# Gram products of a tile in one run, other TensorE work spread over a slot per unit, lookups written straight into the gram operand

## Chip, cores and metric

One core of one Trainium2 chip. The metric is the device time of one execution in microseconds, the median of several runs. TensorE is called PE, VectorE DVE, ScalarE ACT, GpSimd POOL, SyncE SP.

## What is computed

For 2048 samples, 32 table rows of 256 values each are gathered by `ids`; all dot products of two different rows of a sample (496) and 16 dense values make 512 features, and three dense layers follow:

```python
e = jnp.stack([tbl_0[ids[:, 0]], ..., tbl_31[ids[:, 31]]], axis=1)   # [2048, 32, 256]
dots = jnp.einsum('bnd,bmd->bnm', e, e)[:, iu, ju]                   # pairs i < j: 496
h = jnp.concatenate([dots, dense_ctx], axis=1)                       # [2048, 512]
h = jnp.maximum(h @ W_top1 + b_top1, 0.0)                            # 512
h = jnp.maximum(h @ W_top2 + b_top2, 0.0)                            # 256
y = h @ W_top3                                                       # [2048, 1]
```

The tables have 1000, 1250 or 12500 rows; everything is float32.

## The kernel before

**Tiles.** The samples are worked on in 16 tiles of 128. For each tile the kernel needs `turned`: the 32 rows of each sample with the 256 values across the partitions (two chunks of 128), from which `gram` (line 348) forms, for each sample, the products of its 32 rows with 31 of them, 256 small matmuls (512 on PE, as each float32 matmul is issued as two) into two banks of `quad_ps`.

**Two ways into `turned`.** 26 fields come by gather: POOL issues one indirect DMA per field and tile (line 295) into a ring of nine places in `rows`, two fields to a place, called a unit; 13 units make a tile (tile 0 has 15, as three more fields are gathered there). `turn` (line 313) transposes a unit on PE in four steps into a ring of four banks, and ACT or DVE (`ACT_UNITS`) copies the bank into `turned`. The gather of unit n waits until unit n-9 is turned. The other six fields, with 1000 rows each, are looked up: the table stays in SBUF as the sum of a high and a low part (`small`), DVE builds `one_hot` from the ids, and `look_up` (line 326) multiplies both, 32 matmuls for one field and two tiles, into the one bank `look_ps`. ACT copies the bank to `ahead` (line 490), and `place` (line 501) copies it from there into `turned`, twice per tile. There are 48 lookups, three per tile; half the fields come in even tiles, half in odd ones, a tile ahead of their use.

**The split.** In tile 0 ACT writes a table's high part (line 555), copies it to PSUM in four pieces (line 561), and DVE subtracts each piece from the table to get the low part (line 664).

**After gram.** `unfold` (DVE, line 618) moves the products to SBUF, `pick` (ACT, lines 506 to 514) sorts them into `features`, PE transposes these (`turn_features`), `keep_features` copies, then `layer1` (line 407), `keep_hidden1`, `layer2` (line 420) on PE and `last_layers` on DVE.

**Order on PE, written out by hand.** For each tile t: the turns of units 4 to 12, with the features of tile t-1 after unit 6, then layer 1 of tile t-1 (`turn_all`); then eight portions, each a ninth of the tile's lookups followed by an eighth of its gram products; layer 2 of tile t-1 stands after the first portion, and after portions 3 to 6 stand the turns of units 0 to 3 of tile t+1 (`EARLY_AFTER`). A last ninth of the lookups closes the tile. The last tile has a gram of its own (`last_gram`, line 377: 256 matmuls on PE in four banks), and behind it stand its features, layers and the output. ACT, DVE and SP have loops of their own in matching order, bound to PE by semaphores.

Of the kernel before, what the change touches and what calls it, by code (L numbers as in the profile page):

```python
# [8 lines left out]
D = 256  # L9
P = 128  # L10
# [28 lines left out]
def dlrm_tower(nc, dense_ctx, ids, small_ids, tables, w1, b1, w2, b2, w3, out):  # L39
# [30 lines left out]
    ACT_UNITS = [0, 1, 2, 6, 8, 10, 12]  # L70
    RING = 4


    LOOK_AFTER = [2, 5, 8, 11]
    SPLIT_AFTER = [0, 2, 5, 8]

    EARLY_AFTER = [3, 4, 5, 6]

    TURN_FEATURES_AFTER = 6
    PARTS = 8  # L80
    GPP = GROUPS // PARTS
# [7 lines left out]
    AT_ONCE = 2  # L89
    STEPS = SUB // AT_ONCE  # L90
    IDS_RING = 3
    OUTS = 4 * CHUNKS

    LOOKUPS, FIRST = [], {}
    for step in range(-1, TILES):
        FIRST[step] = len(LOOKUPS)
        n = step + 1  # L100
        if step == -1:
            LOOKUPS += [(f, 0, 2) for f in range(EVENS)] + [(EVENS, 1, 2)]
        elif n < TILES and n % 2 == 0:
            LOOKUPS += [(f, n, 2) for f in range(EVENS)]
        elif n < TILES:
            LOOKUPS += [(f, n, min(2, TILES - n)) for f in range(EVENS + (n == 1), SMALL)]
    FIRST[TILES] = len(LOOKUPS)
    PRODUCTS = CHUNKS * SUB * 2

    ctx = ExitStack()  # L110
    with ctx:
# [16 lines left out]
        with nc.sbuf_tensor("landed", [SP, SMALL, SUB, 2, D], fp32) as landed:  # L128
# [4 lines left out]
        ahead = sbuf("ahead", [P, SMALL, CHUNKS, 2 * P])  # L133
# [13 lines left out]
        turn_ps = [psum(f"turn_ps{i}", [P, 512]) for i in range(RING - 2)] + [quad_ps[:, b, :] for b in (2, 3)]  # L147
        look_ps = psum("look_ps", [P, 512])
# [8 lines left out]
        last_h1 = [top_ps, look_ps, turn_ps[0], turn_ps[1]]  # L157
# [7 lines left out]

        high_ps = [bank[0:SP, 0:AT_ONCE * D].rearrange("p (r d) -> p r d", r=AT_ONCE)
                   for bank in (gram_ps[:, 1, :], top_ps)]
# [13 lines left out]
        high_copied = sem("high_copied")  # L181

# [4 lines left out]
        look_kept = sem("look_kept")  # L187
        placed = sem("placed")
# [38 lines left out]
        def n_gathered(n):  # L227

            return 16 * sum(len(UNITS[m][1]) for m in range(n % PLACES, n + 1, PLACES))

# [7 lines left out]
        def _(sp):  # L238
# [71 lines left out]
        def _(pe):  # L310
# [15 lines left out]
            def look_up(n, first, end):  # L326

                f, _, tiles = LOOKUPS[n]
                width = tiles * P
                if first == 0:  # L330
                    pe.wait_ge(one_hot_made, n + 1)
                    if n < SMALL:
                        pe.wait_ge(low_parts, (f + 1) * STEPS)
                    if n > 0:
                        pe.wait_ge(look_kept, n)
                for k in range(first, end):
                    c, r, part = k // (2 * SUB), k // 2 % SUB, k % 2
                    last = pe.matmul(look_ps[:, c * width:(c + 1) * width],  # L338
# [5 lines left out]
            def gram(t, portion):  # L344
                if portion == 0:
                    pe.wait_ge(act_kept, n_act_kept(BEGIN[t + 1] - 1))
                    pe.wait_ge(dve_kept, n_dve_kept(BEGIN[t + 1] - 1))
                    pe.wait_ge(placed, 2 * t + 1)
                    if t > 0:
                        pe.wait_ge(unfolded, t)  # L350
                if t == 0 and portion == PARTS // 2:
                    pe.wait_ge(low_parts, SMALL * STEPS)
                for g in range(portion * GPP, (portion + 1) * GPP):
# [7 lines left out]
                if portion == PARTS - 1:  # L361
                    last.then_inc(gram_done, 1)

            def last_gram(portion):
                t = TILES - 1
# [13 lines left out]
                if (portion + 1) * GPP % LAST_GROUPS == 0:  # L379
                    last.then_inc(last_gram_done, 1)  # L380
# [356 lines left out]
```

## Time and profile before

| | us |
|---|---|
| median of 3 runs | 566.03 (565.94 to 626.95) |
| profiled execution, span | 890.7 |
| PE busy in it | 601.0 |
| POOL busy in it | 398.0 |
| DVE, ACT busy in it | 225.9, 204.6 |

The time of the profiled execution itself is known by its span alone, from the first to the last instruction. A line of the page or of an answer gives an engine, the line of the kernel, the operation, what it writes and reads, how many instructions, and times in us (ns where so marked). "issue" is idle time of an engine for which the profile shows no wait. The span is far longer than the timed runs, which has to be kept in mind with every share.

### The profile page before, as it was taken

The page shows a single profiled execution, that of the slowest core. Times are in us where ns is not written, and L with a number is a line of the kernel's source. Part 1 is how long each engine was busy: PE and PEld are TensorE (multiplying, and loading weights), DVE is VectorE, ACT ScalarE, POOL GpSimd, SP SyncE. Part 2 cuts the span into 40 slices and gives each one's busy share as a digit, 9 for nine tenths or more (in the row PEclk, how much of TensorE's full clock was granted, in tenths as well). Part 3 has the DMA queues.
Part 4 walks back from the last instruction along what each step waited for, and adds up shares of the span by engine and source line. Part 5 has one row for each costly group of instructions (what it writes and reads, how often), then busy time and mean ns, then how long its engine had stood idle before and what let it go on. Part 6 is the DMA issues. An engine that isn't in the chain of part 4 may idle for free.

```text
span 890.7 us, 24184 instructions
## 1 busy us (share of the span) xinstructions
PE 601.0 (67%) x11019; PEld 524.1 (59%) x11019; DVE 225.9 (25%) x578; ACT 204.6 (23%) x369; POOL 398.0 (45%) x426
## 2 busy tenths in 40 slices
PE   3557668486684867748577584875848668486687
PEld 2456557375572756737467474765737657375586
DVE  3444313123130231402223032231312313123122
ACT  4252303103030030401313022130210303103042
POOL 7563625526255361543715347262462625526220
PEclk9688969698796987969789697896969969698799
DMA  9962312313122141321313224131231312313110
GB/s 220 243 204 68 99 42 77 94 44 102 43 78 83 50 107 38 83 73 56 108 37 87 63 57 118 32 96 49 70 105 39 101 41 76 88 41 90 43 38 2
DMA packets 37459, 70.97 MB, mean 80 GB/s; under 512 B 10382, under 2 KB 23438, under 8 KB 37358
## 3 DMA queue, kind: packets, MB, share of 16 engines
q0 software_dynamic: 20112, 54.95, 22.1%
q1 hardware_dynamic: 17246, 14.48, 7.0%
q8 instruction: 87, 1.43, 0.7%
q14 instruction: 14, 0.11, 0.0%
HBM read 69.39 MB, written 0.01 MB: 78 GB/s over the span
## 4 chain that ended last, share of the span: by engine, by line
PE 42%; another core or an unknown queue 30%; issue 13%; ACT 12%; DMA 1%; DVE 1%; POOL 1%; ACTq 0%; DVEq 0%
PE look_ps L338 18%; PE quad_ps L358 12%; PE top_ps L420 6%; ACT turned L501 4%; ACT turned L483 3%; PE turn_ps L322 3%; PE quad_ps L322 2%; ACT area L550 2%; ACT ahead L490 1%; DMA rows<-in_tbl,row_ids 1%; PE quad_ps L377 1%; POOL rows L295 1%; PE top_ps L407 1%; ACT products L506 0%
## 5 line engine op out<-in xcount | busy, mean ns | idle before, releaser
L295 POOL DMA_INDIRECT rows<-in_tbl,row_ids x419 | 397.2, 948 | 458.1 <-PE turn_ps L322 184.1
L338 PE MATMUL look_ps<-one_hot,small 125*128 125x256 f32 (+1 forms) x1536 | 251.9, 303 | 104.7 <-issue 92.8
L338 PEld LDWEIGHTS look_ps<-one_hot,small 125*128 125x128 f32 x1536 | 214.0, 202 | 116.6 <-issue 112.3
L358 PE MATMUL quad_ps<-turned 128*32 128x31 f32 x7680 | 140.0, 204 | 121.8 <-issue 121.5
L358 PEld LDWEIGHTS quad_ps<-turned 128*32 128x32 f32 x7680 | 108.8, 115 | 166.9 <-issue 153.3
L674 DVE TENSOR_SCALAR one_hot<-ids_across,sub_row 125x256 fp32r<-125x256 int32 (+1 forms) x384 | 112.0, 364 | 145.8 <-PE look_ps L338 126.6
L322 PE MATMUL turn_ps<-ident,rows 128*128 128x128 f32 x424 | 64.5, 282 | 28.5 <-issue 14.7
L655 DVE TENSOR_TENSOR top_ps<-top_ps,b_sb 128x256 f32<-128x256 f32 x15 | 6.5, 433 | 299.8 <-PE top_ps L420 299.8
L490 ACT ACTIVATE ahead<-look_ps 128x512 f32<-128x512 f32 (+1 forms) x48 | 28.3, 590 | 232.5 <-PE look_ps L338 219.1
L407 PE MATMUL top_ps<-area,w_sb 128*128 128x128 f32 x488 | 61.9, 276 | 19.5 <-issue 18.8
L550 ACT ACTIVATE area<-top_ps,b_sb 128x128 f32<-128x128 f32 x61 | 17.5, 368 | 227.5 <-remote 225.2
L407 PEld LDWEIGHTS top_ps<-area,w_sb 128*128 128x128 f32 x488 | 57.8, 192 | 18.1 <-issue 17.2
L322 PEld LDWEIGHTS turn_ps<-ident,rows 128*128 128x128 f32 x424 | 48.2, 143 | 31.8 <-issue 28.2
L483 ACT ACTIVATE turned<-turn_ps 128x512 f32<-128x512 f32 x57 | 35.0, 631 | 114.2 <-PE quad_ps L358 76.2
L322 PE MATMUL quad_ps<-ident,rows 128*128 128x128 f32 x414 | 60.1, 279 | 0.8 <-DMA rows<-in_tbl,row_ids 0.8
L483 ACT ACTIVATE turned<-quad_ps 128x512 f32<-128x512 f32 x55 | 33.9, 631 | 90.6 <-PE quad_ps L358 70.8
L420 PE MATMUL top_ps<-w_sb,area 128*128 128x256 f32 x120 | 49.4, 585 | 4.1 <-ACT area L550 4.1
L618 DVE STREAM_TRANSPOSE products<-quad_ps 128x992 f32<-128x992 f32 x15 | 18.3, 1217 | 127.7 <-PE quad_ps L358 127.7
L322 PEld LDWEIGHTS quad_ps<-ident,rows 128*128 128x128 f32 x414 | 46.5, 142 | 2.9 <-DMA rows<-in_tbl,row_ids 1.2
L501 ACT ACTIVATE turned<-ahead 128x768 f32<-128x768 f32 x31 | 45.0, 1552 | 0.0
L420 PEld LDWEIGHTS top_ps<-w_sb,area 128*128 128x128 f32 x120 | 35.6, 311 | 13.9 <-ACT area L550 6.1
L609 DVE COPY turned<-quad_ps 128x512 f32<-128x512 f32 (+1 forms) x49 | 33.0, 681 | 34.1 <-PE quad_ps L322 14.6
(50 smaller groups left out, 169.9 us busy)
## 6 DMA issues: line engine op xcount, KB each, us to landing
rows<-in_tbl,row_ids POOLq DMA_INDIRECT x419
ids_across<-in_small_ids SPq DMA_DIRECT2D x45, 128.0 KB
landed<-in_tbl SPq DMA_DIRECT2D x6, 896.0 KB
w_sb<-in_W_top SPq DMA_DIRECT2D x4, 256.0 KB
landed<-in_tbl SPq DMA_DIRECT2D x6, 104.0 KB
w_sb<-in_W_top SPq DMA_DIRECT2D x1, 512.0 KB
area<-in_dense_ctx SPq DMA_DIRECT2D x16, 8.0 KB
row_ids<-in_ids SPq DMA_DIRECT2D x1, 240.0 KB
```

Source lines behind the costliest of these rows:

```text
L295: pool.indirect_dma_start(out=rows[:, n % PLACES, j, :], out_offset=None, in_=tables[f], in_offset=bass.IndirectOffsetOnAxis(ap=row_ids[:, ...
L322: last = pe.transpose(turn_ps[n % RING][:, at:at + P], rows[:, n % PLACES, j, c * P:(c + 1) * P], ident[:, :])
L338: last = pe.matmul(look_ps[:, c * width:(c + 1) * width], small[:, f, r, part, c * P:(c + 1) * P], one_hot[n % 2][:, r, 0:width], start=(r ...
L358: last = pe.matmul(gram_ps[q * FIELDS:(q + 1) * FIELDS, g // BANK_GROUPS, at:at + COLS], turned[:, c, s, :], turned[:, c, s, 0:COLS], star ...
L407: last = pe.matmul(bank[:, m * P:(m + 1) * P], w1_sb[:, c, m * P:(m + 1) * P], features_t[:, c, :], start=(c == 0), stop=(c == KC - 1))
L420: last = pe.matmul((last_h2 if t == TILES - 1 else top_ps)[:, 0:HIDDEN2], hidden1[:, c, :], w2_sb[:, c, :], start=(c == 0), stop=(c == M1 ...
L483: act.activation(turned[:, :, :, f:f + len(unit)], turn_ps[n % RING][:, 0:CHUNKS * len(unit) * P].rearrange("p (c f s) -> p c s f", c=CHUN ...
L490: act.activation(ahead[:, f, :, 0:tiles * P], look_ps[:, 0:CHUNKS * tiles * P].rearrange("p (c s) -> p c s", c=CHUNKS), ACT.Copy).then_inc ...
L501: act.activation(turned[:, :, :, fs].rearrange("p c s f -> p f c s"), ahead[:, fs, :, half * P:(half + 1) * P], ACT.Copy).then_inc(placed, 1)
L550: act.activation(hidden1[:, m, :], bank[:, m * P:(m + 1) * P], ACT.Relu, bias=b1_sb[:, m:m + 1]).then_inc(h1_kept, 1)
L609: dve.tensor_copy(turned[:, :, :, f:f + len(unit)], turn_ps[n % RING][:, 0:CHUNKS * len(unit) * P].rearrange("p (c f s) -> p c s f", c=CHU ...
L674: last = dve.tensor_scalar(one_hot[n % 2][:, r, 0:width], ids_across[0:SP, n % IDS_RING, 0:width], sub_row[:, r:r + 1], None, ALU.is_equal)
```

## The change

PE's order becomes: for each tile t from 1 on, 13 slots, one per unit. A slot turns the unit, then does its share of the tile's lookups (`SLOT_SHARES`, 96 matmuls in all); slot 2 also transposes the features of tile t-1, slots 5 to 8 do a quarter of layer 1 each, slot 12 does layer 2 (slot 10 in the last tile). Then the gram products of tile t follow in one run. Tile 0 has its turns and three lookups, then gram. Turn banks go from four to three, lookup banks from one to two. A lookup is copied by ACT straight into `turned` for its own tile, and its second tile's half to `ahead`, so that `place` runs once per tile. The split of a small table is one copy on ACT and one subtraction on DVE with both operands in SBUF, spread over tile 0. ACT's, DVE's and SP's loops follow the slots. POOL's program is as before. The core of the diff:

```diff
-    ACT_UNITS = [0, 1, 2, 6, 8, 10, 12]
-    RING = 4
-    EARLY_AFTER = [3, 4, 5, 6]
-    TURN_FEATURES_AFTER = 6
-    PARTS = 8
+    ACT_UNITS = [0, 2, 4, 6, 8, 10, 12]
+    RING = 3
+    LOOKS = 2
+    LOOK_AFTER = [2, 5, 8]
+    HIGH_AFTER = [0, 2, 5, 8, 10, 12]
+    LOW_AFTER = [0, 2, 5, 9, 11, 13]
+    FEATURES_SLOT = 2
+    LAYER1_SLOTS = [5, 6, 7, 8]
+    LAYER2_SLOT = 12
+    LAST_LAYER2_SLOT = 10
+    SLOT_SHARES = [11, 11, 7, 11, 11, 3, 3, 3, 3, 11, 11, 11, 0]
...
+    for t in range(TILES):
+        FIRST[t] = len(LOOKUPS)
+        LOOKUPS += [(f, t, min(2, TILES - t)) for f in (range(EVENS) if t % 2 == 0 else range(EVENS, SMALL))]
...
-            load_ids(5)
             for t in range(TILES):
-                if t + 2 in FIRST:
-                    for n in range(FIRST[t + 1], FIRST[t + 2]):
-                        load_ids(n)
-                if t + 1 < TILES:
-                    load_dense(t + 1)
+                for n in range(FIRST[t], FIRST[t + 1]):
+                    if t > 0 and n == FIRST[t + 1] - 1:
+                        load_dense(t)
+                    if n >= 2 and n + 3 < len(LOOKUPS):
+                        load_ids(n + 3)
...
+            gram(0)
+            for t in range(1, TILES):
+                for i in range(BEGIN[t + 1] - BEGIN[t]):
+                    turn(BEGIN[t] + i)
+                    look_in_slot(t, i)
+                    if i == FEATURES_SLOT:
+                        turn_features(t - 1)
+                    if i in LAYER1_SLOTS:
+                        layer1(t - 1, LAYER1_SLOTS.index(i))
+                    if i == (LAST_LAYER2_SLOT if t == TILES - 1 else LAYER2_SLOT):
                         layer2(t - 1)
-                    if k in EARLY_AFTER and t + 1 < TILES:
-                        turn(BEGIN[t + 1] + EARLY_AFTER.index(k))
-                look_between(t, PARTS)
+                if t < TILES - 1:
+                    gram(t)
+                else:
+                    last_gram()
...
-                act.activation(ahead[:, f, :, 0:tiles * P],
-                               look_ps[:, 0:CHUNKS * tiles * P].rearrange("p (c s) -> p c s", c=CHUNKS),
-                               ACT.Copy).then_inc(look_kept, 1)
+                both = look_ps[n % LOOKS][:, 0:CHUNKS * tiles * P].rearrange("p (c t s) -> p t c s", c=CHUNKS, t=tiles)
+                act.activation(turned[:, :, :, f], both[:, 0, :, :], ACT.Copy).then_inc(look_placed, 1)
+                if tiles == 2:
+                    act.activation(ahead[:, f, :, :], both[:, 1, :, :], ACT.Copy).then_inc(look_kept, 1)
...
-                act.wait_ge(high_ready, i + 1)
-                for k in range(STEPS):
-                    n = i * STEPS + k
-                    if n >= 2:
-                        act.wait_ge(low_parts, n - 1)
-                    act.activation(high_ps[n % 2], small[:, i, k * AT_ONCE:(k + 1) * AT_ONCE, 0, :],
-                                   ACT.Copy).then_inc(high_copied, 1)
...
             def split_low(i):
-                for k in range(STEPS):
-                    n, part = i * STEPS + k, slice(k * AT_ONCE, (k + 1) * AT_ONCE)
-                    dve.wait_ge(high_copied, n + 1)
-                    dve.tensor_tensor(small[:, i, part, 1, :], landed[:, i, part, 1, :], high_ps[n % 2],
-                                             ALU.subtract).then_inc(low_parts, 1)
+                dve.wait_ge(high_ready, i + 1)
+                dve.tensor_tensor(small[:, i, :, 1, :], landed[:, i, :, 1, :], small[:, i, :, 0, :],
+                                  ALU.subtract).then_inc(low_parts, 1)
...
+            for t in range(1, TILES):
+                unfold(t - 1)
+                for i in range(BEGIN[t + 1] - BEGIN[t]):
+                    if i not in ACT_UNITS:
+                        keep_turned(BEGIN[t] + i)
+                    for n in done_in_slot(t, i):
+                        if n + 2 < len(LOOKUPS):
+                            make_one_hot(n + 2)
+                    if t == TILES - 1 and i == LAST_LAYER2_SLOT:
                         last_layers(t - 1)
-                if t == TILES - 1:
+                if t < TILES - 1:
                     last_layers(t - 1)
```

ACT's loop, not shown, does per tile: `place`, then in each slot the unit's copy if it is ACT's, the lookups that ended in that slot, `pick` in slot 0, `keep_features` in slot 2 and `keep_hidden1` in slot 8.

## Rows read from the trace of the kernel before

**Rows 1.** The page's head.
```profile
span 890.7 us, 24184 instructions
```
**Rows 2.** Cores: span and mean granted TensorE clock.
```profile
core 0: 890.7 us, clock 0.850
```
**Rows 3.** List of waits: engine, output, line, releaser; us, times, longest.
```profile
PE quad_ps L358 <- issue: 121.5, 188, 1.9
...
PE look_ps L338 <- issue: 92.8, 103, 2.0
```
**Rows 4.** Stretches: length, busy PE, PEld, DVE, ACT, POOL; clock, DMA share, GB/s.
```profile
377.00:394.00 17.00, 4.88 (x17) 3.33 (x18) 0.82 (x3) 0.60 (x1) 10.84 (x12) 0.63 0.38 107
...
407.00:421.00 14.00, 10.45 (x290) 8.90 (x288) 2.33 (x8) 0.60 (x1) 7.05 (x8) 1.00 0.25 71
```
**Rows 5.** Timeline of POOL: start, us, instruction, idle time before and its releaser.
```profile
2.71 1.10 POOL L295 DMA_INDIRECT rows<-in_tbl,row_ids  x1 [1.15 <-DMA row_ids<-in_ids]
4.12 0.95 POOL L295 DMA_INDIRECT rows<-in_tbl,row_ids  x1 [0.30 <-issue]
...
389.00 0.95 POOL L295 DMA_INDIRECT rows<-in_tbl,row_ids  x1 [0.30 <-issue]
390.25 0.95 POOL L295 DMA_INDIRECT rows<-in_tbl,row_ids  x1 [0.30 <-issue]
406.38 0.94 POOL L295 DMA_INDIRECT rows<-in_tbl,row_ids  x1 [15.19 <-PE turn_ps L322]
...
855.87 0.95 POOL L295 DMA_INDIRECT rows<-in_tbl,row_ids  x1 [0.31 <-issue]
```
**Rows 6.** Timeline of PE, dense stretch of tile 6.
```profile
400.35 0.76 PE L358 MATMUL quad_ps<-turned 128*32 128x31 f32 x64
401.05 1.58 PE L338 MATMUL look_ps<-one_hot,small 125*128 125x256 f32 x11
402.55 0.76 PE L358 MATMUL quad_ps<-turned 128*32 128x31 f32 x64
```
**Rows 7.** Timeline of PE, the last tile.
```profile
862.93 1.04 PE L322 MATMUL turn_ps<-ident,rows 128*128 128x128 f32 x8
863.80 3.74 PE L407 MATMUL top_ps<-area,w_sb 128*128 128x128 f32 x32
867.47 1.15 PE L377 MATMUL quad_ps<-turned 128*64 128x62 f32 x32
868.77 1.99 PE L420 MATMUL top_ps<-w_sb,area 128*128 128x256 f32 x8 [0.15 <-ACT area L550]
870.70 6.75 PE L377 MATMUL quad_ps<-turned 128*64 128x62 f32 x224
```
**Rows 8.** DMA from 855 to 862 us: busy tenths in 40 slices.
```profile
DMA  0030000995100096530000000000000000000000
```
**Rows 9.** Instruction groups by shape: busy us, mean ns of one; idle before.
```profile
L501 ACT ACTIVATE turned<-ahead 128x768 f32<-128x768 f32 x31 | 45.0, 1552 | 0.0
L483 ACT ACTIVATE turned<-turn_ps 128x512 f32<-128x512 f32 x57 | 35.0, 631 | 114.2 <-PE quad_ps L358 76.2 <-remote 24.8 <-PE turn_ps L322 11.3
...
L490 ACT ACTIVATE ahead<-look_ps 128x512 f32<-128x512 f32 x45 | 27.1, 603 | 217.8 <-PE look_ps L338 204.5 <-remote 13.4
...
L512 ACT ACTIVATE area<-products 128x465 f32<-128x465 f32 x15 | 9.2, 612 | 0.5
L664 DVE TENSOR_TENSOR small<-landed,quad_ps 125x512 fp32r<-125x512 f32 x12 | 8.2, 685 | 9.6 <-issue 4.7 <-ACT quad_ps L561 4.5
```
**Rows 10.** Timelines of DVE and POOL: DVE instructions with a gather beside them.
```profile
17.45 0.69 DVE L664 TENSOR_TENSOR small<-landed,quad_ps 125x512 fp32r<-125x512 f32 x1
...
17.87 0.94 POOL L295 DMA_INDIRECT rows<-in_tbl,row_ids  x1 [0.30 <-issue]
...
411.48 2.33 DVE L674 TENSOR_SCALAR one_hot<-ids_across,sub_row 125x256 fp32r<-125x256 int32 x8 [6.55 <-PE look_ps L338]
411.58 1.07 POOL L295 DMA_INDIRECT rows<-in_tbl,row_ids  x1 [0.30 <-issue]
```

More of the change, by code:

```diff
@@ L87, in dlrm_tower @@
     LAST_GROUPS = GROUPS // LAST_BANKS
-    AT_ONCE = 2
-    STEPS = SUB // AT_ONCE
     IDS_RING = 3
-    OUTS = 4 * CHUNKS
     LOOKUPS, FIRST = [], {}
[L98 to L106, printed above, removed]
+    for t in range(TILES):
+        FIRST[t] = len(LOOKUPS)
+        LOOKUPS += [(f, t, min(2, TILES - t)) for f in (range(EVENS) if t % 2 == 0 else range(EVENS, SMALL))]
     FIRST[TILES] = len(LOOKUPS)
     PRODUCTS = CHUNKS * SUB * 2
+    SLOT_ENDS = [sum(SLOT_SHARES[:i + 1]) for i in range(len(SLOT_SHARES))]
     ctx = ExitStack()
@@ L229, in n_gathered, with n_kept, lookups_done, done_in_slot @@
             return 16 * sum(len(UNITS[m][1]) for m in range(n % PLACES, n + 1, PLACES))
+        def n_kept(n):
+            return sum(tiles == 2 for _, _, tiles in LOOKUPS[:n])
+        def lookups_done(t, products):
+            return [n for n in range(FIRST[t], FIRST[t + 1]) if (n + 1 - FIRST[t]) * PRODUCTS <= products]
+        def done_in_slot(t, i):
+            made = (FIRST[t + 1] - FIRST[t]) * PRODUCTS
+            ends = [made * end // SLOT_ENDS[-1] for end in [0] + SLOT_ENDS]
+            return [n for n in lookups_done(t, ends[i + 1]) if n not in lookups_done(t, ends[i])]
         def n_ids(n):
@@ L329, in look_up @@
                 width = tiles * P
+                bank = look_ps[n % LOOKS]
                 if first == 0:
@@ L342, in look_up, with all_in_place, gram @@
                     last.then_inc(looked_up, 1)
[L344 to L353, printed above, removed]
+            def all_in_place(t):
+                pe.wait_ge(act_kept, n_act_kept(BEGIN[t + 1] - 1))
+                pe.wait_ge(dve_kept, n_dve_kept(BEGIN[t + 1] - 1))
+                pe.wait_ge(look_placed, FIRST[t + 1])
+                if t > 0:
+                    pe.wait_ge(placed, t)
+                    pe.wait_ge(unfolded, t)
+            def gram(t):
+                all_in_place(t)
+                for g in range(GROUPS):
                     at = g % BANK_GROUPS * COLS
@@ L360, in gram, with last_gram @@
                                              start=(c == 0), stop=(c == CHUNKS - 1))
[L361 to L365, printed above, removed]
[L366 to L371 removed]
+                last.then_inc(gram_done, 1)
+            def last_gram():
+                all_in_place(TILES - 1)
+                for g in range(GROUPS):
                     at = g % LAST_GROUPS * WIDE
@@ L427, in keep_running, with look_in_slot @@
                     pe.matmul(spare_ps[:, :], ident[:, :], w1_sb[:, 0, :], start=True, stop=True)
-            def turn_all(t):
-                for i in range(len(EARLY_AFTER), BEGIN[t + 1] - BEGIN[t]):
-                    turn(BEGIN[t] + i)
-                    if i == TURN_FEATURES_AFTER:
-                        turn_features(t - 1)
-                for m in range(M1):
-                    layer1(t - 1, m)
-            def look_between(t, k):
-                made = FIRST[t + 1] - FIRST[t]
-                for n in range(made):
-                    begin, end = (n * (PARTS + 1) + made - 1) // made, ((n + 1) * (PARTS + 1) + made - 1) // made
-                    if begin <= k < end:
-                        look_up(FIRST[t] + n, PRODUCTS * (k - begin) // (end - begin),
-                                PRODUCTS * (k + 1 - begin) // (end - begin))
+            def look_in_slot(t, i):
+                made = (FIRST[t + 1] - FIRST[t]) * PRODUCTS
+                begin, end = (made * at // SLOT_ENDS[-1] for at in ([0] + SLOT_ENDS)[i:i + 2])
+                for n in range(FIRST[t], FIRST[t + 1]):
+                    base = (n - FIRST[t]) * PRODUCTS
+                    first, stop = max(begin - base, 0), min(end - base, PRODUCTS)
+                    if first < stop:
+                        look_up(n, first, stop)
             pe.wait_ge(ident_ready, 1)
```

113 lines of the change are left out of this document (35 added, 78 removed).

## The prediction

> **What bounds the kernel now.** I read the page's head first. The profiled execution spans 890.7 us and the median of the timed runs is 566.03, so 324.7 us of the profile are not in the timed runs, and differences inside the profile cannot be carried over as they stand [rows 1]. The list of waits says where they are: PE sat idle with nothing to wait for ("issue") for 121.5 us before gram products and 92.8 us before lookups [rows 3]. The table of stretches shows it inside one tile: from 377 to 394 us PE is busy 4.88 of 17 us at a granted clock of 0.63, and from 407 to 421 us 10.45 of 14 at 1.00 [rows 4]. I take these stalls to come with the recording and rebuild the time from stretches without them.
>
> Two engines could set the end. The Pool queue's timeline: in every unbroken stretch a gather starts 1.25 us after the one before it (389.00, 390.25), 0.95 busy and 0.30 between. It stops only where it waits for a turn that frees a place in `rows`; the 15.19 us before 406.38 is such a wait, and behind it stands the stalled PE [rows 5]. There are 419 gathers: 29 for tile 0, 26 for each later one. A later tile so costs Pool at least 26 x 1.25 = 32.5 us.
>
> PE's tile at the rates of its dense stretches: 52 transposes of 13 units at 0.87 us per 8 = 5.7; four for the features 0.4; layer 1 from 863.80 to 867.47 = 3.7; layer 2 from 868.77 to 870.70 = 1.9 [rows 7]; 96 lookups at 1.50 per 11 = 13.1; eight gram portions at 0.70 = 5.6 [rows 6]. Sum 30.4 us, which is 2.1 under Pool's 32.5.
>
> The whole time by Pool: the first gather starts at 2.71; with 1.41 to the second, the last starts at 2.71 + 1.41 + 417 x 1.25 = 525.4. In the trace the last gather is issued at 855.87 [rows 5], and the view of DMA from 855 to 862 us has its last busy slice (the 18th of 0.175 us) ending at 858.15: landing 2.3 us after the start [rows 8]. So 527.7, the last unit's turn 0.44, layer 1 3.67, then 890.7 - 867.47 = 23.2 for the rest [rows 1, 7]. Sum 555.0. The median is 11.0 above it. Part of that may lie around the span, between launch and end, part may be gaps in Pool's queue; no row divides it.
>
> So I hold that in the timed runs the gathers set the pace and PE waits about 2 us in each tile for the last unit to land.
>
> **Does Pool stay unbroken before?** Gather of unit n needs turn n-9. With E the end of a tile's last gather, layer 1 and four portions (2.2 us each, layer 2 in the first) bring the first early turn to about E + 1.05 + 0.44 + 3.7 + 10.7 + 0.44 = E + 16.3, and Pool asks for it at E + 22.5; the fourth follows at E + 24.3 for E + 30. Some 6 us are spare.
>
> **The change, part by part.**
> *Gram in one run, turns and lookups in 13 slots.* The count of PE instructions is the same. A slot with 11 lookups is 0.44 + 1.50 = 1.94 us, the 13 slots are 30.4 - 5.6 = 24.8, then gram 5.6. Units land every 2.5 us, so PE catches up behind each gram and waits at the end of the tile, now in small pieces. Gram ends near E + 1.05 + 0.44 + 1.9 + 5.6 = E + 9.0 and the next tile's first turn at E + 9.4, where Pool asks at E + 22.5: 13 us spare instead of 6. Worth nothing while Pool was unbroken. If it was not, it is worth what the gaps were, at most the 11.0. I take nothing.
>
> *A ring of three turn banks and two lookup banks.* A turn waits for the copy three units back: 0.63 us long [rows 9], at least three slots of 1.77 us earlier even while PE catches up. A lookup no longer waits for the copy of the one before. Both lie under Pool: nothing. Without that cover a missed copy would cost PE up to 0.63 per unit, 8 us a tile.
>
> *Lookups straight into `turned`.* ScalarE now makes two copies of 256 elements (0.4 to 0.7 us each, between half the 512-element copy's rate and that of `place`, 1552 ns per 768 [rows 9]) in place of one, and one `place` per tile in place of two. Per tile before 3 x 0.6 + 2 x 1.55 = 4.9, after at most 3 x 1.4 + 1.55 = 5.8, of 32.5 us. Behind it queue `keep_turned` and `pick`; `place`, the first turn copy and `pick` (four copies, the longest 0.61) take at most 1.55 + 0.63 + 2.4 = 4.6 us after gram, and `turn_features` asks after 1.94 + 1.94 + 1.4 = 5.3. Covered: nothing.
>
> *SP's queue.* The id lists are still asked for three lookups ahead and the dense block at the tile's last lookup; behind the dense load's wait for `turn_features` (slot 2) stands one id list that is wanted three lookups, a whole tile, later. Nothing. `make_one_hot` moves between VectorE's turn copies: 8 instructions, 2.33 us [rows 10], less than one unit of Pool, three times a tile. Nothing.
>
> *Layers leave the end.* In the last tile layer 1 of tile 14 (3.67) stood between the last turn and the last gram, and layer 2 (1.93) inside that gram. Now they sit in slots 5 to 8 and 10. What comes in their place: the copy of the last unit, formerly under layer 1, now bare (0.63 and about 0.2 to be seen = 0.85). And slot 10 grows to 0.44 + 1.50 + 1.93 = 3.87, with slot 11 5.81 us where two units land in 5.0: 0.8 late. 3.67 + 1.93 - 0.85 - 0.8 = 4.0 us saved (3.95, rounded). This is on the path.
>
> *The split of the small tables.* Before, ScalarE copied the high part to PSUM in four pieces and VectorE subtracted four times (685 ns each, one operand in PSUM). Now VectorE subtracts once, 2048 elements, at most 4 x 0.685 = 2.74 us [rows 9], six times, all during tile 0. Both operands lie in SBUF, a form that the trace of before never shows beside a gather. Lower bound of what it costs Pool: nothing, since the PSUM form runs beside gathers that stay at 0.94 to 0.95 (17.45 and 17.87). Upper bound: Pool stands still throughout, 6 x 2.74 = 16.4 us. The nearest row is a VectorE instruction fed from SBUF alone: where `make_one_hot` starts at 411.48, the gather at 411.58 takes 1.07 instead of 0.95 [rows 10]. I take 0.12 six times = 0.7 us. The Trainium skill speaks against this edit ("SBUF — State Buffer", Who interferes with whom): a VectorE instruction with two SBUF inputs contends with a GpSimd instruction that reads SBUF, and the later of the two is blocked outright, though the same section infers that descriptor writing escapes. By the strict reading the sum would be that of the upper bound, by the inference that of the lower; no row here decides.
>
> **Sum.** Against the rebuilt 555.0: -4.0 + 0.7 = 551.7. The 11.0 us stay, as Pool's program is untouched: 562.7 us, 0.6% under the median.
>
> **Rivals.**
> *Pool was broken before* (0.20). PE's dense 30.4 is near 32.5; a little more per tile in truth, and early turns would come late. Then the change gives the gaps back, at most all 11.0: 551.7. For it: the two sums are 2.1 us apart, and PE is the one engine whose rate the profile disturbs. Against it: the 6 us of spare, and that some of the 11.0 should lie around the span, where nothing can be given back.
> *The split holds Pool* (0.10). Place: tile 0, six subtractions. 566.0 - 4.0 + 16.4 = 578.4. It decides from 4.0 / 6 = 0.67 us per split: above that the kernel is slower than before. For it: the gather stretched to 1.07. Against it: that is an eighth of a gather, not a standstill, and the subtractions of before left the gathers beside them at their length.
> *PE's clock drops as it idles in every slot* (0.04). It decides where the mean granted clock falls under 30.4 / 32.5 = 0.94. At the profile's mean of 0.850 [rows 2] PE's tile is 35.8, 3.3 over Pool: 14 x 3.3 = 46, so 608. Against it: from 407 to 421 us PE was idle a quarter of the time at 1.00 [rows 4], and here it idles one part in fifteen.
> *The change does nothing* (0.04): the end is not shortened because PE reaches the last tile late. 566 to 570.
>
> **How the numbers follow.** Forecast 562.7 us, chance 0.62, its own range 557 to 568. About 2% is what a measurement can tell from no change: under 554.7 is faster, over 577.4 slower. Faster 0.20 (the first rival), same 0.66 (forecast and the last), slower 0.14 (the split, the clock). For 8 in 10 the range takes in the first rival and most of the way to the second: 550 to 575.
>
> **What the profile after would show.** Gathers still 1.25 us apart where unbroken, and none longer than 1.1 beside the new subtraction (2.1 to 2.7 us long): else the second rival. The last gram following the last turn within about 1 us, with no layer 1 or 2 behind it, and some 21.3 us from its start to the end of the span, formerly 23.2. Granted clock at 1.00 wherever PE is not stalled. A time at or under 552 would mean that Pool did not set the pace before; one over 578 that the split or PE's order does so now. The weakest point is that the bound is inferred from rates inside a profile that ran 1.57 times as long as the runs.

## The result and the profile after

The changed kernel takes 650.41 us (646.25 to 654.98, four runs), the kernel before 565.99 beside it: 84.4 us more. The ratio of the fast runs is 1.1527 [1.1458, 1.1596]; it leaves out one run of the kernel before that took 626.95 us (the medians as they stand give 1.149). The prediction said 562.7 and no change; it was wrong. The profiled execution of the changed kernel took 654.98 us, 1.8 more than its span; the other three took 646 to 651, so the loss is not that of one recording.

From the page of the kernel after: the span, the engines' busy time (PEld is PE's weight loads), the queue q8 that carries instructions (packets, MB, share), and the chain that ended last by engine.

```profile
span 653.2 us, 24171 instructions
PE 534.5 (82%) x11019; PEld 507.8 (78%) x11019; DVE 230.5 (35%) x560; ACT 187.5 (29%) x374; POOL 407.8 (62%) x426
q8 instruction: 87, 1.43, 0.9%
PE 78%; issue 15%; POOL 5%; DMA 1%; DVE 0%; ACT 0%; DVEq 0%
```

PE carries the chain, and 15% of the chain is PE idle with no wait that the profile shows. The list of waits (total us, times, longest) says where; it answers to [rows 3]:

```profile
PEld quad_ps L362 <- issue: 104.5, 111, 3.7
PE quad_ps L362 <- issue: 84.8, 47, 3.3
POOL rows L296 <- PE turn_ps L323: 61.2, 34, 6.8
```

L362 is the gram run; 47 idle times, 84.8 us, of which 3.3 stand ahead of the first run and 81.5 inside the 15 runs. PE's timeline over one run and the start of the next tile (start, length, instructions, idle before); it answers to [rows 6]:

```profile
319.64 1.89 PE L418 MATMUL top_ps<-w_sb,area 128*128 128x256 f32 x8
321.46 2.64 PE L362 MATMUL quad_ps<-turned 128*32 128x31 f32 x181
325.78 2.14 PE L362 MATMUL quad_ps<-turned 128*32 128x31 f32 x128 [1.68 <-issue]
329.79 1.93 PE L362 MATMUL quad_ps<-turned 128*32 128x31 f32 x128 [1.86 <-issue]
333.24 1.28 PE L362 MATMUL quad_ps<-turned 128*32 128x31 f32 x75 [1.52 <-issue]
334.45 1.12 PE L323 MATMUL turn_ps<-ident,rows 128*128 128x128 f32 x4
335.22 2.69 PE L341 MATMUL look_ps<-one_hot,small 125*128 125x256 f32 x11
```

The run takes 12.99 us, where the prediction had 5.6. Its first 181 matmuls take 2.64 us, 0.93 per 64 where the prediction had 0.70, and from the 181st on it stops after exactly 128 matmuls each time. Each matmul has a weight load of its own, so 128 matmuls are 256 instructions; and q8 moves 1.43 MB in 87 packets, 16 KB each, against 2 x 11019 matmuls and weight loads, 253 to a packet. Four of these packets fall into this run ("q8 instruction: 4, 0.07, 2.3%" in the view of DMA from 321.46 to 334.45).

The table of stretches: us, then busy time with instructions of PE, PEld, DVE, ACT and POOL, then granted clock, DMA share and GB/s. The rows are the slots before the run, the run, the start of the slots behind it, and the rest of those.

```profile
299.65:321.46 21.81, 21.81 (x175) 21.32 (x174) 10.86 (x29) 7.91 (x17) 16.16 (x17) 0.95 0.41 115
321.46:334.45 12.99, 7.73 (x513) 6.95 (x513) 1.34 (x6) 0.00 (x0) 6.65 (x7) 0.66 0.37 97
334.45:342.00 7.55, 7.55 (x50) 7.55 (x48) 1.91 (x2) 3.75 (x7) 4.25 (x5) 0.69 0.20 55
342.00:359.65 17.65, 17.65 (x148) 17.16 (x147) 10.35 (x29) 7.24 (x16) 13.38 (x15) 1.00 0.44 121
```

PE stops, and the granted clock is at its lower level (1.2 GHz of 2.4) for part of the run and of what follows: 0.66 in the mean of the run, 0.69 in the 7.55 us behind it, 1.00 after that. The 11 lookups at 335.22 take 2.49 us to the next start instead of the 1.50 of [rows 6]. Over 15 tiles the run lasts 13.3 us in the mean, with three stops (four in one run), 5.4 us, in it; the slots between two runs last 24.8. Together 38.1 us a tile against POOL's 32.5 [rows 5]: 15 x 5.6 = 84 us, as much as the measured difference. POOL now waits for PE in nearly every tile:

```profile
329.23 0.95 POOL L296 DMA_INDIRECT rows<-in_tbl,row_ids  x1 [0.30 <-issue]
335.84 0.95 POOL L296 DMA_INDIRECT rows<-in_tbl,row_ids  x1 [5.67 <-PE turn_ps L323]
```

### The profile page after: what moved, and what is told of

It reads as the page before. It is cut to its first block, busy times and chain, and to the rows that moved or that the text cites. A ratio compares the mean times of both kernels' runs of the same rounds, so it can differ in the third digit from the quotient of the medians.

```text
span 653.2 us, 24171 instructions
## 1 busy us (share of the span) xinstructions
PE 534.5 (82%) x11019; PEld 507.8 (78%) x11019; DVE 230.5 (35%) x560; ACT 187.5 (29%) x374; POOL 407.8 (62%) x426
## 3 DMA queue, kind: packets, MB, share of 16 engines
q8 instruction: 87, 1.43, 0.9%
## 4 chain that ended last, share of the span: by engine, by line
PE 78%; issue 15%; POOL 5%; DMA 1%; DVE 0%; ACT 0%; DVEq 0%
PE quad_ps L362 17%; PE quad_ps L341 15%; PE look_ps L341 14%; PE turn_ps L323 10%; PE top_ps L405 9%; PE quad_ps L323 5%; POOL rows L296 5%; PE top_ps L418 4%; PE quad_ps L375 1%; PE top_ps L395 1%; DMA rows<-in_tbl,row_ids 1%; PE turn_ps L405 0%; PE quad_ps L418 0%; DMA row_ids<-in_ids 0%; DVE products L607 0%
## 5 line engine op out<-in xcount | busy, mean ns | idle before, releaser
L362 PE MATMUL quad_ps<-turned 128*32 128x31 f32 x7680 | 115.1, 219 | 88.3 <-issue 84.8
L362 PEld LDWEIGHTS quad_ps<-turned 128*32 128x32 f32 x7680 | 100.2, 131 | 106.3 <-issue 104.5
L341 PE MATMUL look_ps<-one_hot,small 125*128 125x256 f32 (+1 forms) x768 | 130.1, 316 | 0.0
L341 PE MATMUL quad_ps<-one_hot,small 125*128 125x256 f32 (+1 forms) x768 | 127.4, 311 | 0.0
L341 PEld LDWEIGHTS look_ps<-one_hot,small 125*128 125x128 f32 x768 | 112.6, 216 | 0.0
L341 PEld LDWEIGHTS quad_ps<-one_hot,small 125*128 125x128 f32 x768 | 110.0, 212 | 0.0
L323 PE MATMUL turn_ps<-ident,rows 128*128 128x128 f32 x560 | 95.5, 298 | 17.3 <-DMA rows<-in_tbl,row_ids 17.3
L583 DVE COPY turned<-turn_ps 128x512 f32<-128x512 f32 x65 | 45.3, 697 | 123.8 <-PE turn_ps L323 123.6
L323 PEld LDWEIGHTS turn_ps<-ident,rows 128*128 128x128 f32 x560 | 71.4, 153 | 19.8 <-issue 11.4
L491 ACT ACTIVATE turned<-ahead 128x768 f32<-128x768 f32 x15 | 23.3, 1555 | 214.6 <-PE quad_ps L362 214.6
L418 PE MATMUL top_ps<-w_sb,area 128*128 128x256 f32 x120 | 28.4, 380 | 0.0
```

The costliest lines, as they stand in the source:

```text
L323: last = pe.transpose(turn_ps[n % RING][:, at:at + P], rows[:, n % PLACES, j, c * P:(c + 1) * P], ident[:, :])
L341: last = pe.matmul(bank[:, c * width:(c + 1) * width], small[:, f, r, part, c * P:(c + 1) * P], one_hot[n % 2][:, r, 0:width], start=(r == ...
L362: last = pe.matmul(gram_ps[q * FIELDS:(q + 1) * FIELDS, g // BANK_GROUPS, at:at + COLS], turned[:, c, s, :], turned[:, c, s, 0:COLS], star ...
L418: last = pe.matmul((last_h2 if t == TILES - 1 else top_ps)[:, 0:HIDDEN2], hidden1[:, c, :], w2_sb[:, c, :], start=(c == 0), stop=(c == M1 ...
L491: act.activation(turned[:, :, :, fs].rearrange("p c s f -> p f c s"), ahead[:, fs, :, :], ACT.Copy).then_inc(placed, 1)
L583: dve.tensor_copy(turned[:, :, :, f:f + len(unit)], turn_ps[n % RING][:, 0:CHUNKS * len(unit) * P].rearrange("p (c f s) -> p c s f", c=CHU ...
```

## The experiments

The theory that they test: PE's instructions arrive in blocks of 256 (128 short matmuls) at a pace of about one block in 3.7 us, and a run of short matmuls uses them up faster. Rivals: the slots and lookups, the split of the tables, or the end are the cause; or the stops belong to the start of a run. The comparisons stand beside the kernel before on the same chip: 563.98 us for e1 to e4, 562.67 for e5 to e8, 563.82 for e9 and e10, 562.65 for e11 (medians of 9 to 17 runs, which spread over 3 to 7 us). The kernels of e1 to e3, e6 to e8 and e10 were run once each.

### e1: the kernel before, again

No edit; its first profile spans 890.7 us, with PE held up [rows 1, 3, 4].

> The kernel before, unchanged, profiled once more. Theory (the recording stalled the first profile; the timed runs are dense): span about 564 us, PE's idle time marked issue far under the 248 us of the first profile, a tile every 32.5 to 33.5 us, and the gathers 1.25 us apart nearly without a break. Rival (a tile of the kernel before takes the 54.6 us of the first profile in every recorded run): span near 890 us again.

Measured: 559.83 us. The page's head; POOL's last gathers; PE around two portions of gram:

```profile
span 558.0 us, 24184 instructions
PE 507.1 (91%) x11019; PEld 466.4 (84%) x11019; DVE 231.4 (41%) x578; ACT 203.7 (37%) x369; POOL 397.6 (71%) x426
```

```profile
526.54 0.95 POOL L295 DMA_INDIRECT rows<-in_tbl,row_ids  x1 [0.30 <-issue]
527.79 0.95 POOL L295 DMA_INDIRECT rows<-in_tbl,row_ids  x1 [0.30 <-issue]
```

```profile
312.61 0.99 PE L358 MATMUL quad_ps<-turned 128*32 128x31 f32 x64
313.52 1.57 PE L338 MATMUL look_ps<-one_hot,small 125*128 125x256 f32 x11
315.02 0.99 PE L358 MATMUL quad_ps<-turned 128*32 128x31 f32 x64
```

The gathers run unbroken at 1.25 us (2.3 us of gaps in all), so POOL sets the pace, as the prediction held. A portion of 64 with its 11 lookups is 150 instructions in 2.41 us, 62 per us. A block of 256 per 3.7 us is 69 per us. The kernel before lies just under what the supply gives. What held PE up in its first profile is not shown: there PE stops after every one or two matmuls, not 256 instructions apart.

### e2: the kernel before with its gram portions in one run

```diff
-                for k in range(PARTS):
+                for k in range(PARTS + 1):
                     look_between(t, k)
+                    if t > 0 and k == 0:
+                        layer2(t - 1)
+                for k in range(PARTS):
                     if t < TILES - 1:
                         gram(t, k)
...
+                if t + 1 < TILES:
+                    for i in range(len(EARLY_AFTER)):
+                        turn(BEGIN[t + 1] + i)
```

> The kernel before with one thing of the change alone: the lookups of a tile come first, then its gram products in one run, then the four early turns. Lookup path, banks, split and everything else as before. Theory (a run of 512 gram matmuls outruns the supply of PE's instructions): gram takes 12 to 14 us per tile instead of some 6 with stops of 1.7 to 2.2 us after every 128 matmuls, the clock falls to 1.2 GHz behind it, and the time is 640 to 680 us. Rival (slots, three turn banks or the new lookup copies cost the 84 us): about 566 us, at most 575.

Measured: 794.08 us. PE's and POOL's timelines:

```profile
301.31 2.18 PE L358 MATMUL quad_ps<-turned 128*32 128x31 f32 x234
305.74 1.29 PE L358 MATMUL quad_ps<-turned 128*32 128x31 f32 x128 [2.25 <-issue]
309.20 1.93 PE L358 MATMUL quad_ps<-turned 128*32 128x31 f32 x128 [2.16 <-issue]
```

```profile
314.79 0.94 POOL L295 DMA_INDIRECT rows<-in_tbl,row_ids  x1 [16.55 <-PE turn_ps L322]
```

The same stops with the lookup path, banks and split of before: the run in one piece is enough. The size was missed. Here the early turns come only behind the run, the nine places of `rows` fill, and POOL waits for PE 247 us in all, some 16 us a tile; in the changed kernel it is 91 us, some 6 a tile.

### e3: the kernel after with half as many, wider gram instructions

```diff
...
-                        for q in range(QUADS):
-                            s = q * FIELDS + g
-                            last = pe.matmul(gram_ps[...], turned[:, c, s, :], turned[:, c, s, 0:COLS],
+                        for h in range(HALVES):
+                            s = QUADS * g + 2 * h
+                            pair = turned[:, c, s:s + 2, :]
+                            last = pe.matmul(quad_ps[...], pair.rearrange("d s f -> d (s f)"), pair[:, :, 0:COLS],
```

It takes two samples to one matmul, as the last tile does, and writes the products of one half of the samples over those of the other.

> The changed kernel with gram of tiles 0 to 14 in the form of the last tile's: 256 matmuls of 62 columns in place of 512 of 31, so half the instructions in one run, with more array time (7.7 us instead of 4.3). Results of different samples are written over each other, so the output is not the reference's. Theory (instruction supply): no stops of over 1 us within gram, gram 7.7 to 8.5 us, clock back at 2.4 GHz, a tile of some 32.5 us set by the gathers or just above, 555 to 585 us. Rival (the products themselves, the clock or the wait for data make the run slow): gram stays at 12 us or over and the time at 640 us or over.

Measured: 564.82 us.

```profile
314.57 7.68 PE L363 MATMUL quad_ps<-turned 128*64 128x62 f32 x256
```

No stop inside a run, the granted clock at 1.00 in the run shown, tiles of 32.5 us, and the whole loss is gone with the slots, direct lookups, rings and split of the change all in place. The run's 512 instructions (256 matmuls and as many weight loads) take 7.6 us, 67 per us, just under the 69 of the supply. The one thing altered is the number and length of the gram instructions.

### e4: the kernel before with the new split

One copy on ACT and one subtraction on DVE per table, in the places of the old ones (`AT_ONCE` 8, the copies to PSUM left out).

> The kernel before with the new split alone: one copy on ACT and one subtraction on DVE with both operands in SBUF per small table, at the places of before. In the changed kernel's trace the six gathers beside these subtractions took 2.17 to 2.72 us instead of 0.95, 8.9 us in all. Theory that gathers set the pace of the kernel before from its first tile on: 5 to 10 us slower than before (570 to 576). Rival (gathers have spare time in the kernel before, PE sets its pace): within 2 us of before, or faster, as ACT loses 14 us of copies in tile 0.

Measured: 567.32 us (six runs), ratio 1.0062 [1.0036, 1.0088]: 3.5 us, between the two theories. In the profile six gathers of tile 0 take 1.9 to 3.0 us instead of 0.95, and the last gather starts at 536.05 instead of 527.79. The same rows in the kernel after, POOL and then the subtraction (ns, shortest, median, longest):

```profile
14.24 0.95 POOL L296 DMA_INDIRECT rows<-in_tbl,row_ids  x1 [0.30 <-issue]
15.50 2.58 POOL L296 DMA_INDIRECT rows<-in_tbl,row_ids  x1 [0.30 <-issue]
```

```profile
L636 DVE TENSOR_TENSOR small<-landed,small x6: 2267/2283/2293, 15.0 to 51.2; 125x2048 fp32r<-125x2048 f32 x6
```

### e5: the kernel before with the layers of tile 14 ahead of the last turns

In the last tile layer 1 stands behind unit 10 and layer 2 behind unit 11.

```diff
+                    if t == TILES - 1 and i == 10:
+                        for m in range(M1):
+                            layer1(t - 1, m)
+                    if t == TILES - 1 and i == 11:
+                        layer2(t - 1)
...
```

> The kernel before with one thing of the change: in the last tile layer 1 of tile 14 goes ahead of the turns of units 11 and 12, and layer 2 between these two turns, instead of behind them. In the second profile of the kernel before, PE waits 1.81 us there for the last unit to land, then does layer 1 (3.66 us) and, inside the last gram, layer 2 (1.92 us). Theory (gathers set the pace up to the last unit): some 3.5 to 5 us faster than before, 559 to 561. Rival (PE is late in the last tile anyway): within 1 us of before.

Measured: 562.23 us (twelve runs), ratio 0.9987 [0.9959, 1.0015]: no difference to be measured.

```profile
528.57 3.74 PE L407 MATMUL top_ps<-area,w_sb 128*128 128x128 f32 x32
532.14 0.60 PE L322 MATMUL turn_ps<-ident,rows 128*128 128x128 f32 x4
533.54 1.99 PE L420 MATMUL top_ps<-w_sb,area 128*128 128x256 f32 x8 [0.79 <-ACT area L556]
535.37 0.60 PE L322 MATMUL turn_ps<-ident,rows 128*128 128x128 f32 x4
```

The last gather starts at 528.58, so its rows have landed near 531, but PE reaches the last turn at 535.37: the layers only push the turns back. PE had too little idle time in the last tile for them to fall into.

### e6, e7: the dose

`PARTS` 4 and 2 in the kernel before, portions of 128 and 256 matmuls with correspondingly more lookups between, the early turns placed anew. (e7 lets PE wait for `place` before the first lookup of a tile.)

> The kernel before with gram in 4 portions of 128 matmuls per tile instead of 8 of 64, lookups between them in larger pieces. Theory (PE has some 190 gram matmuls in stock at the start of a run, then gets 128 every 3.7 us): a portion fits the stock, no stops over 1 us, 560 to 572 us. Rival (each product in a longer run is slower from the start, or the clock falls with any run): in proportion to the run, a quarter of the way from 564 to the 794 of one run, 600 us or over.

> The kernel before with gram in 2 portions of 256 matmuls per tile; PE also waits for the tile's copies and placements ahead of its first lookup. Theory (stock of some 190, then 128 every 3.7 us): about one stop of 1.5 to 2.2 us in each portion, 3 to 4.5 us more per tile with a little low clock, of which about 1 us is hidden under the gathers: 595 to 640 us. Rival (supply is no matter below a whole tile's run): 564 to 575 us.

Measured: 565.56 and 601.71 us. PE's idle time by "issue" before gram products is 5.7 us in e6 (6 times); in e7 it is

```profile
PE quad_ps L358 <- issue: 42.8, 28, 2.4
```

e7's tiles take 33 to 38 us. With one portion (e2) it is 794. What counts is how many short matmuls stand together: portions of 64 and 128 show no cost beyond the spread of the runs, 256 do.

### e8: the kernel after with the layers inside the run

The four parts of layer 1 and layer 2 of tile t-1 move from the slots into the gram run, behind groups 9, 13, 17, 21 and 27 of 32.

> The changed kernel with layer 1 in four pieces and layer 2 put between the gram products (after groups 9, 13, 17, 21 and 27 of 32) in tiles 1 to 14, and no longer in slots 5 to 8 and 12. Same work, same instructions. Theory (PE's instructions are short in the run): PE fetches on while the 40 layer matmuls keep it busy for 5.3 us, so the stops shrink from 6 us per tile to 1 to 3 and a tile from 38.1 to 33 to 35.5 us: 570 to 615 us. Rival (the stops are waits for data or banks, not supply): the stops stay at 6 us and the time at 640 to 655 us.

Measured: 592.95 us. PE's idle time by "issue" in the run falls from 84.8 us (47 times) to 29.9:

```profile
PE quad_ps L362 <- issue: 29.9, 27, 3.1
```

Tiles take 32 to 36 us. The work is the same and only its order differs.

### e9, e11: an attempt at a version that beats both

e9 is the kernel after with the split of before, two lookup products of the next tile behind each group of 16 gram matmuls, and layers and three turns among the groups. e11 goes back to eight portions of 64, with six lookup products behind each, layer 1 ahead of the run, and layers in the slots in the last tile alone. From e11's edit, the run:

```diff
...
+                    if (g + 1) % GPP == 0:
+                        k = g // GPP
+                        look_early(t + 1, IN_RUN * k // PARTS, IN_RUN * (k + 1) // PARTS)
+                        if t > 0 and k == LAYER2_PART:
+                            layer2(t - 1)
+                        if k in TURN_PARTS:
+                            turn(BEGIN[t + 1] + TURN_PARTS.index(k))
+                look_early(t + 1, IN_RUN, 2 * PRODUCTS)
...
```

> The kernel after, with the split of the kernel before, and with long instructions between the gram products: after each of the 32 groups of 16 matmuls stand two lookup products of the next tile, and among the groups the four parts of layer 1, layer 2 and three turns of the next tile; in the slots one lookup is left. Theory (PE's instructions are supplied at a fixed rate, and the run of short matmuls drains the stock): PE gets no stops, its tile is 30.4 us, POOL stays unbroken with the last gather at about 528 us, and the short end of the kernel after (26.7 us from the last gather to the end in the run with pairs, against 30.2 before) stays: span 554 to 557, time 556 to 559, about 1% faster than before. Rival 1 (the end is bound otherwise, as in the run with layers moved in the last tile): 562 to 566. Rival 2 (the stops belong to the gram products themselves, whatever stands between): 600 to 650.

Measured: 832.72 us (six runs, 817.39 to 834.58), far outside all three. PE's timeline:

```profile
319.09 0.33 PE L367 MATMUL quad_ps<-turned 128*32 128x31 f32 x16
319.35 0.51 PE L344 MATMUL look_ps<-one_hot,small 125*128 125x256 f32 x2
319.79 0.33 PE L367 MATMUL quad_ps<-turned 128*32 128x31 f32 x16
343.43 1.11 PE L409 MATMUL top_ps<-ident,area 128*128 128x128 f32 x4 [3.27 <-ACT area L513]
356.97 0.33 PE L367 MATMUL quad_ps<-turned 128*32 128x31 f32 x16 [2.30 <-DVE turned L601]
```

The stops are gone, not one over 0.5 us inside a run, as the supply would have it. But a group with its two lookups takes 0.70 us at the full clock (319.09 to 319.79), where the rates of [rows 6] give 16 x 0.70 / 64 + 2 x 1.50 / 11 = 0.45: by this comparison a change of kind and back costs some 0.25 us, 32 times a tile. The run so takes 31 us; ahead of it PE waits 2.3 us for the last copy, behind it 3.3 us for `pick` (39.5 and 48.7 us over the whole execution, of the 269 lost), and POOL stands still four times a tile (tiles of 48 to 54 us). The mean granted clock is 0.82. How much of the rest the changes, the clock and the order of the turns each make was not separated.

> The kernel after with the split of the kernel before and its gram run broken again into eight portions of 64 matmuls; behind each portion stand six lookup products of the next tile, behind the third also layer 2 and behind the fourth to sixth a turn of the next tile; layer 1 stands ahead of the run and covers the copy of the last unit, a half lookup behind it covers the move of the products to SBUF; the last tile has its layers in the slots, as in the kernel after. Theory (the run alone made the kernel after slow; with portions POOL is the bound again): no stops of PE, gathers unbroken to about 528 us, from there to the end 26 to 28 us instead of 30: 556 to 561 us, ratio 0.985 to 0.998. Rival 1 (the switches between kinds of matmul, seen as 0.25 us per pair in the run with two products behind each group, push PE over POOL's 32.5 us per tile): 565 to 590. Rival 2 (the shorter end is taken up by PE reaching the last tile late): 562 to 566.

Measured: 581.35 us (six runs), ratio 1.0311 [1.0261, 1.0361].

```profile
303.68 0.90 PE L370 MATMUL quad_ps<-turned 128*32 128x31 f32 x64
304.51 0.98 PE L347 MATMUL quad_ps<-one_hot,small 125*128 125x256 f32 x6
305.42 0.73 PE L370 MATMUL quad_ps<-turned 128*32 128x31 f32 x60
307.23 0.25 PE L370 MATMUL quad_ps<-turned 128*32 128x31 f32 x4 [1.09 <-issue]
```

Portions of 64 as in the kernel before, but six lookups between them instead of 11: 140 instructions in 1.74 us (303.68 to 305.42), 80 per us, more than 69, and the stops are back, in nine of the portions over 0.5 us. They are the smaller part, though: PE's list of waits has 9.8 us of "issue" in all and 26.4 us for DVE's copies into `turned`, 19.2 of it before turns:

```profile
PE turn_ps L329 <- DVE turned L613: 10.9, 10, 2.5
```

Tiles take 32.4 to 34.3 us, over POOL's 32.5, and PE reaches the last tile late (last gather 545.5, last turn 557.9). No version here beats the kernel before.

### e10: the gram run twice as long

```diff
-                for g in range(GROUPS):
+                for g in [*range(GROUPS), *range(GROUPS)]:
```

> The kernel after, with every product of the gram run issued twice over (the second pass starts its sums anew, so the values are the same), in 15 of the 16 tiles: 1024 matmuls in a run instead of 512. Theory (instructions come in blocks of 256, one block per 3.6 to 3.7 us, and a stock of about 190 matmuls stands at the start): the second half runs at the pace of the supply alone, 4 x 3.66 = 14.6 us more per tile, 15 x 14.6 = 220 more, 860 to 885 us in all, with seven stops a run, each 128 matmuls after the one before. Rival (the stops are a cost of the start of a run, or of the clock climbing): the second half runs at the dense 0.70 to 0.96 us per 64, 5.6 to 7.7 us more per tile, 735 to 770 us.

Measured: 873.15 us.

```profile
319.08 2.95 PE L362 MATMUL quad_ps<-turned 128*32 128x31 f32 x201
324.29 2.07 PE L362 MATMUL quad_ps<-turned 128*32 128x31 f32 x128 [2.26 <-issue]
327.74 1.95 PE L362 MATMUL quad_ps<-turned 128*32 128x31 f32 x128 [1.39 <-issue]
331.47 1.93 PE L362 MATMUL quad_ps<-turned 128*32 128x31 f32 x128 [1.78 <-issue]
...
341.85 1.93 PE L362 MATMUL quad_ps<-turned 128*32 128x31 f32 x128 [1.54 <-issue]
345.59 0.97 PE L362 MATMUL quad_ps<-turned 128*32 128x31 f32 x55 [1.81 <-issue]
```

Seven stops, each 128 matmuls behind the one before, to the end of the run: it is a pace and not a cost of the start. From 324.29 to 345.59 six blocks take 3.55 us each; over all runs of e10 the mean is 3.71, in the kernel after 3.78. In the second half of e10's runs no gather starts (POOL waits about 20 us a tile), and the pace stays, so the gathers do not make it.

Three things in the traces tie the stops to PE's code. First, e10 issues 7680 matmuls more than the kernel after, 15360 instructions with their weight loads, and q8 moves 60 packets more, one for each 256; e3 issues 7680 instructions fewer and q8 moves 30 packets fewer, 57. In e10:

```profile
q8 instruction: 147, 2.41, 1.1%
```

Second, where the stops stand: with PE's matmuls, weight loads and semaphore instructions numbered from the start, all 267 stops of over 0.5 us by "issue" in the kernel after, e2, e6, e7, e8, e10 and e11 (but for four in tile 0, ahead of or early in its work) stand at number 192 or 193 modulo 256. So they belong to fixed places in PE's program, 256 instructions apart, whichever kernel it is. That is why the first stop of a run comes after anything from 127 to 249 matmuls, and at the same matmul, run for run, in e10 (1024 instructions more in a tile, four times 256) as in the kernel after. The fixed stock of some 190 matmuls that the expectations of e6, e7 and e10 speak of is only the mean of these: the first such place in a run is passed, and PE stops at the second.

Third, the packets themselves. In the run of the kernel after shown above, packets of q8 end at 324.39, 328.28 and 331.88, and the stops end at 325.78, 329.79 and 333.24; the next packets start at 326.90, 330.89 and 334.36. Every one of the 267 stops ends 1.2 to 1.6 us after the end of a packet, the next packet starts at least 1.0 us after PE has gone on, and no two packets of q8 overlap. About 1.3 us to the packet, 1.0 for it and 1.4 from it to PE make the 3.7 us. So the stops are PE waiting for the next block of its code. No run changed the supply itself.

## Why the prediction was wrong, by its steps

**What bounds the kernel before: right.** Last gather 527.79 in e1, forecast 525.4; span 558.0, rebuilt 555.0; the time is 1.8 us above the span. The first rival (Pool broken before) falls for this run: 2.3 us of gaps, not 11.0. Of the 11.0 us that no row divided, 3.0 lie in the span and 1.8 around it. The other 6.2 stay open: e1 is shorter than every other run of this kernel on its chip (559.83 against 562.35 to 565.45), and no trace shows a run of this kernel near its median.

**PE's 30.4 us a tile: too low.** The portion of 64 takes 0.81 us in the mean of e1, not 0.70, as the rows of [rows 6] were from its fast end. PE was 91% busy, so it had less to spare than the sum said.

**Gram in one run: the step that failed.** "The count of PE instructions is the same" is true and beside the point; "then gram 5.6" carried a rate over from 64 matmuls in a row to 512. The run takes 13.3 us, 5.4 of them stops in which PE waits for its instructions, the rest the work, at more than 0.70 per 64 and partly at the lower clock. The term was 7.7 us too small in each of 15 tiles, which turns "under Pool's 32.5" into 38.1. e3 takes the stops away and the loss goes with them; e2, e7 and e10 bring them by the length of the run (e2 and e7 move lookups and early turns with it). The page of before had the signs: 87 packets of instructions against 22,000 matmuls and weight loads on PE, and no row with more than 64 short matmuls together. With PE 5.6 us a tile behind Pool, the 13 us of spare for Pool's turns are gone within the first tiles: Pool's first wait of over 1 us for PE ends at 106.6 us.

**Rings, direct lookups, SP's queue, one-hots: right at nothing, taken together.** In the kernel after ACT and DVE are busy 29% and 35% and wait for PE; e3, which holds all of these, is at 564.82. No run takes them one by one.

**Layers leave the end: right in place, without worth here.** The end of the kernel after:

```profile
630.92 0.62 PE L323 MATMUL quad_ps<-ident,rows 128*128 128x128 f32 x4
632.23 7.68 PE L375 MATMUL quad_ps<-turned 128*64 128x62 f32 x256 [0.69 <-ACT turned L474]
```

From the last gram to the end of the span 21.0 us, forecast 21.3, and 1.3 from the last turn to it, forecast 0.44 + 0.85. With POOL as the bound (e3) the end from the last gather is 26.7 us against 30.2 in e1. But it needs a PE that keeps up: in e5 and e11 PE comes late to the last turn.

**The split: mis-sized.** 0.12 us for each was read from a one-hot with one operand in SBUF. Beside the new subtraction the gather takes 2.2 to 2.7 us instead of 0.95 in the kernel after, six of six, 8.9 us in all against the 0.7 taken and the 16.4 of the upper bound. Hidden in the kernel after, 3.5 us where POOL is the bound (e4). By the Trainium skill ("SBUF — State Buffer", Who interferes with whom) a VectorE instruction with two SBUF inputs contends with a GpSimd instruction that reads SBUF, and the trace agrees. The inference of that section that descriptor writing escapes did not save these gathers, which also read their row ids from SBUF; which of the two is held up was not separated.

**The rivals and the range.** The rival "PE's clock drops" named a symptom with the wrong cause: the mean clock is 0.851, close to the 0.850 it was priced at, but PE does not idle in the slots, it stops in the run, and the time is 42 us above the 608 of that rival. A run of gram at the pace of something other than PE was on no list, and so the range ended 75 us too low. The sign named for the second rival, a gather of over 1.1 us beside the new subtraction, came six times; still the split is not the cause, as e3 holds it and is at 564.82.

## What to carry to other kernels

A rate read from short bursts of small instructions is not the rate of a long run of them: before gathering small matmuls into one run, count how many stand together in any row of the trace, and work out instructions per microsecond over the stretch. Here the limit was about 69 per us: where PE got through 256 instructions in less than some 3.7 us, a stop followed, except at the first such place of a run. Interleaving longer instructions, or fewer and wider ones, keeps under it. An interleaving that looks untidy may be what pays for this, and where it is made too fine each change of kind seems to cost as well (some 0.25 us a pair in e9).

## What the runs showed of the hardware

- **PE's instructions come at a pace.** Blocks of 256 in 3.7 to 3.8 us in the mean, 14 to 15 ns per instruction, while a dense portion of 64 matmuls uses one per 5.5 ns (0.70 us for 128). A stop ends 1.2 to 1.6 us after a 16 KB packet of q8 has ended. The first stop of a run comes after 127 to 249 matmuls, by where the run stands in PE's program. By the Trainium skill ("Runtime: NRT & Kernel Launch", Instruction fetch mechanics) instructions are fetched in blocks of 16 KiB, 256 instructions, and the cost of crossing into the next one is mostly hidden. The size agrees; the cost is not hidden here.
- **The clock follows the stops.** The granted clock is 0.66 in a run with three stops and 0.69 in the 7.55 us behind it, and there the same 50 matmuls take 7.4 us (334.45 to 341.86) against 5.3 in e3 (322.18 to 327.47): 2.1 us in this tile beyond the stops, 1.8 in the mean.
- **Changing between kinds of matmul seems to cost PE some 0.25 us a pair** (e9: 16 of 128*32 tiles and two of 125*128 by turns take 0.70 us, the separate rates give 0.45). No run varied the number of changes alone.
